# A fused decoder layer on one core: router work of the first token half two rounds earlier, last normalisations on ScalarE, router work of the second half one expert later

## The chip, the core and the metric

The kernel runs on one core of a Trainium2 chip. The time is the device time of one execution in microseconds (us). TensorE is called PE here, VectorE DVE, ScalarE ACT, GpSimd POOL and SyncE SP, as in the profile. Each engine runs its own list of instructions in order; they meet only at semaphores (a `then_inc` by one, a `wait_ge` by another).

## The reference, cut to what matters

```python
x = x + attn(layernorm(x))                       # local attention, blocks of 12 tokens
x = x + xattn(layernorm(x), ctx_1024)            # 16 heads, 512 context tokens, rope on the keys
x = x + ffn(layernorm(x))                        # the part that the change touches

def ffn(x, P_w, U1, U2, U3, W1, W2, b2):         # 1024 tokens of 128, 12 experts, top 3 of 12
    x_addr = x @ P_w.T                           # 64 wide
    dw1, dw2, dw3 = (route(x_addr @ U.T, 3) for U in (U1, U2, U3))   # softmax over the 3 largest
    h = sum(x @ W1[e].T * dw1[:, e:e+1] for e in range(12))          # 512 wide
    y = sum(gelu(h) @ W2[e].T * dw2[:, e:e+1] for e in range(12))
    return y + dw3 @ b2
```

The layer norms are over the last axis, without weights; the tokens are 4 batches of 256.

## The kernel before, in words

The 1024 tokens lie as 8 tiles of 128 in `x_sb`. After the local attention comes the cross attention: 4 batches times 16 heads, two heads at a time, so 32 **rounds** (`for r in range(NPAIR)`, one such loop on PE, ACT, DVE and POOL). A round r does, on PE and in this order: the scores of the next pair (L1075), a tile of values of a later group (`unit`, L901, up to round 27), in even rounds the queries of a later group (L1018 to L1020), the values weighed (L1092), the sum of weights (L1102), in some rounds (19, 21, 27, 29) a projection (L1111), a tile of keys (`unit`, L901, up to round 24) and the keys of pair r + 3 turned (L1004). ACT takes two exponentials (L749), copies the value tile (L670), the queries (L741) and the keys (L729). DVE divides the pair before (L1488, L1492), clips (L1481, two), and turns the key tile with rope (L1371, L1376). POOL sums the weights over key tiles (L519 two, L525 one) and adds the rope halves (L511).

Value tiles and key tiles, and the router, share one bank, 5, of the accumulator memory. So before its next use PE waits for the reader of the last: `rope_done` of DVE's L1376 after keys, `v_done` of ACT's L670 after values.

The last part is a mixture of experts on two halves of 512 tokens. The loop over n from 0 to 23 takes half 0 with its experts 0 to 11 and then half 1: `first_mixture(n)` (L1234 to L1236, 12 matmuls). Its input is made by DVE (`xeT`, L1520), ACT (`xeT_hi`, L763) and POOL (`xeT_lo`, L550, `token_rest`). Half 0 is ready for the final layer norm while the cross attention still runs, since its batches are done; half 1 is ready only after the projection of the last batch, which PE does behind `first_mixture(0)`.

Before a half can enter the mixture it goes through the **router**: statistics on DVE (`final_norm(half, 0)`, L1308, L1311), the reciprocal root on POOL (`rstd_of`, L468, L469), the normalisation (`final_norm(half, 1)`, L1314 on DVE), and stages `tokens` (4 transposes, L1154), `address` (L1158), `scores` (L1162, and on DVE the three largest), `chosen` and `softmax` (DVE), `turn` (4 transposes, L1167, then copies on ACT and DVE, and `gate_src`, which SP stores and spreads). A table `ROUTE` gives the half round of each stage for half 0, `ROUTE_2` the number n for half 1; an even entry 2r lies on PE ahead of the weighing of values of round r, an odd one at the end of the round. With the constants here `LAST_KEYS` is 24, so `ROUTE` runs from 49 (`weights`, the end of round 24) over 50, 52, 54, 56, 58 to 60 (round 30). `NORM_ROUND` is 23: statistics of half 0 in round 23, normalisation in round 24. On PE each stage in `ROUTE` first waits for `v_done` of the newest value tile; `weights` also waits for `rope_done` of all 32 key tiles:

```python
if i in ROUTE.values():
    pe.wait_ge(s["v_done"], min(i // 2 + V_LEAD, NG * KC - 1) + 1)
if i == ROUTE["weights"]:
    pe.wait_ge(s["rope_done"], NG * KC)
```

In half 1 POOL runs `token_rest(0)`, then `rstd_of`, then `token_rest(1)` and the rest, while DVE takes the statistics at n = 0 and normalises at n = 1.

Of the kernel before, what the change touches and what calls it, by code (L numbers as in the profile page):

```python
# [7 lines left out]
P = 128  # L8
# [15 lines left out]
def decoder_layer(nc, x, ctx_in, pos, a_wq, a_wk, a_wv, a_wpost, a_wrel, a_pds,  # L24
# [75 lines left out]
    with ExitStack() as ctx:  # L100
# [37 lines left out]
        def bank(i, parts=P):  # L138
# [10 lines left out]
        NSTAT = LN_F + NT  # L149
        stats = sb("stats", [P, NSTAT, 6])  # L150
# [121 lines left out]
            z_done fill_done top_done top3_done zr_done chosen_done zsh_done ez_done wsel_done zsum_done zrec_done  # L272
# [50 lines left out]
        def pv_bank(p):  # L323
# [5 lines left out]
        ROUTE = {"weights": 2 * LAST_KEYS + 1, "tokens": 2 * LAST_KEYS + 2, "address": 2 * LAST_KEYS + 4, "scores": 2 * LAST_KEYS + 6,  # L329
                 "chosen": 2 * LAST_KEYS + 8, "softmax": 2 * LAST_KEYS + 10, "turn": 2 * LAST_KEYS + 12}  # L330
        ROUTE_READ = {"weights": ("rt_done", 2), "tokens": ("fT_done", 1), "address": ("addr_done", 1), "scores": ("z_done", 1)}
        FILLED = 20
        NORM_ROUND = (B - 1) * PPB - 1

        ROUTE_2 = {"tokens": 3, "address": 4, "scores": 5, "chosen": 6, "softmax": 7, "turn": 8}

        HIDDEN = {NE: [(0, range(0, HC // 2))], NE + 1: [(0, range(HC // 2, HC))], 2 * NE - 1: [(1, range(HC))]}
        BIAS = {1: ("turn", 0), 2: ("product", 0), 9: ("turn", 1), 10: ("product", 1)}
# [117 lines left out]
        def _(pool):  # L456
# [102 lines left out]
            for r in range(NPAIR):  # L559
                for b, rounds in LATENT_ROUNDS.items():  # L560
                    for part in range(2):
                        if r == rounds[part]:
                            rstd_of(LN_1 + (2 * b + part) * TPB, TPB)
                if r + 1 < NPAIR:
                    weights_summed(2 * r + 2)
                    weights_summed(2 * r + 3)
                    halves_summed(r + 1)
                if r in ROUND_KEYS:
                    key_sum(r + K_LEAD)
                if r == NORM_ROUND:  # L570
                    rstd_of(LN_F, NT // 2)
                if r == FILLED:
                    pool.wait_ge(s["x1_done"], NT)
                    pool.memset(z[:, :, NE:NE + FILL], LOWEST).then_inc(s["fill_done"], 1)
                    pool.memset(top3[:, :, TOPK:8], LOWEST).then_inc(s["fill_done"], 1)
                    pool.memset(dw1T[:, :].bitcast(F32), 0.0).then_inc(s["fill_done"], 1)
                    pool.tensor_tensor(pick[:, :], ident[0:SPLIT, 0:NE], ident[0:SPLIT, REST:SPLIT], ALU.add).then_inc(s["pick_done"], 1)
                    pool.wait_ge(s["pick_done"], 1)
                    pool.tensor_copy(spread[:, :, :], pick[:, 0:GE, None].to_broadcast([SPLIT, GE, P])).then_inc(s["spread_done"], 1)

            token_rest(0)
            rstd_of(LN_F + NT // 2, NT // 2)
            for n in range(1, 2 * NE):
                token_rest(n)

        @block.scalar
        def _(act):
# [176 lines left out]

            def route(half, stage, at):
# [39 lines left out]
            for r in range(NPAIR):  # L805
# [24 lines left out]
            for n in range(2 * NE):  # L830
# [22 lines left out]
        def _(pe):  # L853
# [315 lines left out]

            def route_1(i):  # L1170
                if i in ROUTE.values():
                    pe.wait_ge(s["v_done"], min(i // 2 + V_LEAD, NG * KC - 1) + 1)
                if i == ROUTE["weights"]:
                    pe.wait_ge(s["rope_done"], NG * KC)
# [10 lines left out]
            for r in range(NPAIR):  # L1185
# [6 lines left out]
                if r in ROUND_VALUES:  # L1192
                    for stage, (read, count) in ROUTE_READ.items():
                        if ROUTE[stage] in (2 * r - 2, 2 * r - 1):
                            pe.wait_ge(s[read], count)
# [14 lines left out]
                if r in ROUND_KEYS:  # L1210
                    unit(ROUND_KEYS[r])
# [84 lines left out]
        def _(dve):  # L1296
# [225 lines left out]
            def final_norm(half, part):  # L1522
# [6 lines left out]
                else:  # L1529
                    dve.wait_ge(s["rstd_done"], 2 + B + 2 * B + half + 1)  # L1530
                    for i in range(4):
                        t = 4 * half + i
                        normalize(xn[:, t, :], x_sb[:, t, :], LN_F + t).then_inc(s["fn_done"], 1)
# [30 lines left out]
            def route_softmax(half):  # L1564
# [3 lines left out]
                dve.tensor_tensor(chosen[:, :, :], chosen[:, :, :], ez[:, :, :], ALU.mult).then_inc(s["wsel_done"], 1)  # L1568
                dve.wait_ge(s["wsel_done"], half + 1)
                dve.tensor_reduce(zsum[:, :], chosen[:, :, :], AX_X, ALU.add).then_inc(s["zsum_done"], 1)  # L1570
                dve.wait_ge(s["zsum_done"], half + 1)
                dve.reciprocal(zsum[:, :], zsum[:, :]).then_inc(s["zrec_done"], 1)
                dve.wait_ge(s["zrec_done"], half + 1)
# [26 lines left out]
            for r in range(NPAIR):  # L1600
                if r:
                    divide(r - 1)
                if r == NPAIR - 1:
# [20 lines left out]
                if r == NORM_ROUND:  # L1624
                    final_norm(0, 0)
                if r == NORM_ROUND + 1:
                    final_norm(0, 1)
                if r in ROUND_KEYS:
                    key_unit(ROUND_KEYS[r])
                route_1(2 * r + 1)  # L1630
# [3 lines left out]
            for n in range(2 * NE):  # L1634
# [4 lines left out]
                if n == 0:  # L1639
                    dve.wait_ge(s["tail_ps"], 1)  # L1640
                    for t in range(TPB):
                        tile = TPB * (B - 1) + t
                        dve.tensor_tensor(x_sb[:, tile, :], psum[:, 7, t * D:(t + 1) * D], x_sb[:, tile, :], ALU.add)\
                           .then_inc(s["x2_done"], 1)
                    final_norm(1, 0)
                if n == 1:
# [56 lines left out]
```

## Time and profile before

| | us |
|---|---|
| median of 3 runs (477.15 to 481.71) | 477.53 |
| the profiled execution | 475.94 |
| its span (first to last instruction) | 474.2 |
| PE busy in the span | 436.7 |
| DVE, POOL, ACT busy | 327.5, 244.6, 188.6 |

Everything that follows is read from the one profiled execution; positions are in us from the start of its span. PE is the engine on which nearly all of the chain that ended last lies (73% of it), so a row that shows PE idle shows time that the kernel loses, and a row of another engine matters if PE waits for it. A row of the timeline gives start, duration, engine, line, operation, what it writes and reads, and in square brackets how long the engine was idle just before and who ended that. The granted clock (PEclk) is 1.00 at the upper of its two levels, 2.4 GHz, and 0.50 at the lower, 1.2 GHz; a stretch in between held both.

### The profile page before, as it was taken

The page shows a single profiled execution, that of the slowest core. Times are in us where ns is not written, and L with a number is a line of the kernel's source. Part 1 is how long each engine was busy: PE and PEld are TensorE (multiplying, and loading weights), DVE is VectorE, ACT ScalarE, POOL GpSimd, SP SyncE. Part 2 cuts the span into 40 slices and gives each one's busy share as a digit, 9 for nine tenths or more (in the row PEclk, how much of TensorE's full clock was granted, in tenths as well). Part 3 has the DMA queues.
Part 4 walks back from the last instruction along what each step waited for, and adds up shares of the span by engine and source line. Part 5 has one row for each costly group of instructions (what it writes and reads, how often), then busy time and mean ns, then how long its engine had stood idle before and what let it go on. Part 6 is the DMA issues. An engine that isn't in the chain of part 4 may idle for free.

```text
span 474.2 us, 8559 instructions
## 1 busy us (share of the span) xinstructions
PE 436.7 (92%) x3264; PEld 321.7 (68%) x3264; DVE 327.5 (69%) x688; ACT 188.6 (40%) x296; POOL 244.6 (52%) x217
## 2 busy tenths in 40 slices
PE   3975899999999999989997989879999999999996
PEld 2653676766666766657765667558767788888885
DVE  8767578979998577896878579945553642465444
ACT  7648055546445454453443524314345432300000
POOL 5774138996898768877877544633332342000000
PEclk9999999999999999999998999998999999999999
DMA  6764321000000000000000000231425220000000
GB/s 167 183 143 70 60 85 45 0 1 1 0 1 2 1 1 1 0 1 2 1 1 2 1 0 1 80 123 45 134 82 187 103 98 0 3 11 7 11 6 11
DMA packets 32809, 19.83 MB, mean 42 GB/s; under 512 B 16437, under 2 KB 29674, under 8 KB 32770
## 3 DMA queue, kind: packets, MB, share of 16 engines
q1 hardware_dynamic: 32068, 19.02, 14.7%
q8 instruction: 26, 0.43, 0.4%
q10 hardware_dynamic: 702, 0.28, 0.2%
q14 instruction: 13, 0.11, 0.1%
HBM read 17.27 MB, written 2.02 MB: 41 GB/s over the span
## 4 chain that ended last, share of the span: by engine, by line
PE 73%; DVE 15%; ACT 6%; issue 4%; POOL 1%; DVEq 0%; ACTq 0%; POOLq 0%
PE psum L1092 10%; PE psum L1075 10%; PE psum L901 9%; PE psum L1271 5%; PE psum L1272 5%; PE psum L1270 5%; PE psum L1234 4%; PE psum L1236 4%; PE psum L1235 4%; PE psum L1111 3%; PE psum L1004 3%; PE psum L1102 2%; DVE rden L1488 2%; DVE kM L1383 2%; PE psum L1128 1%
## 5 line engine op out<-in xcount | busy, mean ns | idle before, releaser
L519 POOL TENSOR_TENSOR e_part<-e_sb 128x512 f32<-128x512 f32 x64 | 88.3, 1396 | 39.1 <-DVE e_sb L1481 39.1
L749 ACT ACTIVATE e_sb<-psum 128x1024 f32<-128x1024 f32 x64 | 62.4, 1023 | 22.2 <-PE psum L1075 22.2
L1075 PE MATMUL psum<-q_t,kT 64*128 64x256 f32 x512 | 65.6, 396 | 0.0
L1092 PE MATMUL psum<-e_sb,v_sb 128*64 128x256 f32 x512 | 62.9, 385 | 0.0
L1481 DVE TENSOR_SCALAR e_sb<-e_sb 128x1024 f32<-128x1024 f32 x64 | 56.1, 910 | 5.8 <-ACT e_sb L749 5.8
L1488 DVE RECIPROCAL rden<-psum 128x256 f32<-128x256 f32 x32 | 55.9, 1746 | 4.7 <-PE psum L1102 4.7
L1667 DVE SCALAR_TENSOR_TENSOR x_sb<-psum,dw,x_sb 128x128 f32<-128x128 f32 x96 | 33.7, 351 | 36.1 <-PE psum L1272 33.5
L550 POOL TENSOR_TENSOR xeT_lo<-xeT,xeT_hi 128x512 fp32r<-128x512 f32 x24 | 30.9, 1291 | 51.2 <-ACT xeT_hi L763 51.2
L1075 PEld LDWEIGHTS psum<-q_t,kT 64*128 64x128 f32 x512 | 48.1, 191 | 9.8 <-issue 5.4
L729 ACT ACTIVATE kT<-psum 128x512 f32<-128x512 f32 x32 | 19.2, 599 | 87.8 <-PE psum L1004 87.8
L511 POOL TENSOR_TENSOR k_rot<-rope_a,rope_b 128x512 f32<-128x512 f32 x32 | 42.3, 1322 | 16.8 <-DVE rope_b L1376 16.8
L1092 PEld LDWEIGHTS psum<-e_sb,v_sb 128*64 128x64 f32 x512 | 34.3, 136 | 21.4 <-issue 5.8
L1234 PE MATMUL psum<-xeT_hi,w1T_hi 128*128 128x512 f32 x96 | 40.3, 419 | 3.9 <-POOL xeT_lo L550 3.9
L525 POOL TENSOR_TENSOR e_part<-e_part 128x512 f32<-128x512 f32 x32 | 41.3, 1292 | 2.5
L1236 PE MATMUL psum<-xeT_hi,w1T_lo 128*128 128x512 f32 x96 | 38.4, 400 | 0.0
L1235 PE MATMUL psum<-xeT_lo,w1T_hi 128*128 128x512 f32 x96 | 38.1, 397 | 0.0
L1271 PE MATMUL psum<-w2T_lo,h_hi 128*128 128x512 f32 x96 | 38.0, 396 | 0.0
L763 ACT ACTIVATE xeT_hi<-xeT 128x512 fp32r<-128x512 f32 x24 | 15.1, 632 | 57.2 <-DVE xeT L1520 34.4
L1272 PE MATMUL psum<-w2T_hi,h_lo 128*128 128x512 f32 x96 | 37.8, 394 | 0.0
L1371 DVE TENSOR_TENSOR rope_a<-psum,cos_sb 128x512 f32<-128x512 f32 x32 | 22.0, 686 | 22.3 <-PE psum L901 21.9
L1270 PE MATMUL psum<-w2T_hi,h_hi 128*128 128x512 f32 x96 | 37.3, 389 | 0.0
L901 PE MATMUL psum<-wkv_hi,ctx_hi 128*128 128x512 f32 x64 | 31.5, 492 | 4.7 <-DVE rope_b L1376 4.7
(191 smaller groups left out, 778.0 us busy)
## 6 DMA issues: line engine op xcount, KB each, us to landing
w_raw<-in_L_ffn_W_dram SPq DMA_DIRECT2D x24, 256.0 KB, 2.7
gates<-gate_dram SPq DMA_DIRECT2D x6, 768.0 KB, 4.5
ctx_sb<-in_ctx_dram SPq DMA_DIRECT2D x4, 256.0 KB, 6.3
vbd<-v_dram SPq DMA_DIRECT2D x16, 52.6 KB
v_dram<-v_tok SPq DMA_DIRECT2D x4, 136.0 KB, 3.2
raw<-in_L_xattn_Wkv_dram SPq DMA_DIRECT2D x2, 256.0 KB, 5.6
k_rot<-in_L_xattn_Wkv_dram SPq DMA_DIRECT2D x2, 256.0 KB, 4.7
k_rot<-in_L_xattn_Wq_dram SPq DMA_DIRECT2D x2, 256.0 KB, 5.6
```

What stands on the lines that cost most here:

```text
L519: pool.tensor_tensor(e_part[:, p % 2, half, :, :], e_sb[:, i % ERING, :, 0, :], e_sb[:, i % ERING, :, 1, :], ALU.add)\
L749: act.activation(e_sb[:, i % ERING, :, :, :].rearrange("p a k t -> p (a k t)"), psum[:, a:a + 2, :].rearrange("p a b -> p (a b)"), ACT.Exp ...
L901: mm = pe.matmul(o, c, w_[:, wc:wc + GC], start=(part == 0), stop=(part == 2))
L1075: mm = pe.matmul(psum[:, 2 * (i % 2) + a, t * S:(t + 1) * S], kT[rows, p % 3, kt * P:(kt + 1) * P], q_t[rows, j % 2, p % 2, :], start=True ...
L1092: mm = pe.matmul(psum[DX * a:DX * a + DX, pv_bank(p), 0:S], v_sb[g % 2][:, kt, 2 * pp + a, :], e_sb[:, i % ERING, a, t, :], start=(kt == 0 ...
L1234: pe.matmul(bank(c), w1T_hi[:, e, c, :], hi, start=(e == 0), stop=False)
L1235: pe.matmul(bank(c), w1T_hi[:, e, c, :], lo, start=False, stop=False)
L1236: mm = pe.matmul(bank(c), w1T_lo[:, e, c, :], hi, start=False, stop=(e == NE - 1))
L1270: pe.matmul(o, hi, w_hi, start=(c == 0), stop=False)
L1271: pe.matmul(o, hi, w_lo, start=False, stop=False)
L1272: mm = pe.matmul(o, lo, w_hi, start=False, stop=(c == HC - 1))
L1488: dve.reciprocal(rden[:, p % 2, :], psum[:, pv_bank(p), S:2 * S]).then_inc(s["rden_done"], 1)
```

## The change

The diff, cut to its core (the rest renames three semaphores into one, adds the tile `nm` of 128 x 8 and moves a loop into a function):

```diff
-        ROUTE = {"weights": 2 * LAST_KEYS + 1, "tokens": 2 * LAST_KEYS + 2, "address": 2 * LAST_KEYS + 4, "scores": 2 * LAST_KEYS + 6,
-                 "chosen": 2 * LAST_KEYS + 8, "softmax": 2 * LAST_KEYS + 10, "turn": 2 * LAST_KEYS + 12}
+        NORM_ROUND = (B - 1) * PPB - 2
+        ROUTE = {"weights": 2 * NORM_ROUND, "tokens": 2 * NORM_ROUND + 2, "address": 2 * NORM_ROUND + 4, "scores": 2 * NORM_ROUND + 6,
+                 "chosen": 2 * NORM_ROUND + 8, "softmax": 2 * NORM_ROUND + 10, "turn": 2 * NORM_ROUND + 12}
-        NORM_ROUND = (B - 1) * PPB - 1
-        ROUTE_2 = {"tokens": 3, "address": 4, "scores": 5, "chosen": 6, "softmax": 7, "turn": 8}
+        ROUTE_2 = {"tokens": 4, "address": 5, "scores": 6, "chosen": 7, "softmax": 8, "turn": 9}
-        BIAS = {1: ("turn", 0), 2: ("product", 0), 9: ("turn", 1), 10: ("product", 1)}
+        BIAS = {1: ("turn", 0), 2: ("product", 0), 10: ("turn", 1), 11: ("product", 1)}
...
+                if r == NORM_ROUND:
+                    rstd_of(LN_F, NT // 2)
                 if r in ROUND_KEYS:
                     key_sum(r + K_LEAD)
-                if r == NORM_ROUND:
-                    rstd_of(LN_F, NT // 2)
...
-            token_rest(0)
-            rstd_of(LN_F + NT // 2, NT // 2)
-            for n in range(1, 2 * NE):
+            for n in range(2 * NE):
                 token_rest(n)
+                if n == 2:
+                    rstd_of(LN_F + NT // 2, NT // 2)
...
+            def final_normalize(half):
+
+                act.wait_ge(s["nm_done"], half + 1)
+                for t in range(4 * half, 4 * half + 4):
+                    act.activation(xn[:, t, :], x_sb[:, t, :], ACT.Identity, scale=rstd[:, LN_F + t:LN_F + t + 1], bias=nm[:, t:t + 1])\
+                       .then_inc(s["fn_done"], 1)
...
                 route_1(2 * r + 1)
+                if r == NORM_ROUND:
+                    final_normalize(0)
...
+                if n == 3:
+                    final_normalize(1)
...
                 if i == ROUTE["weights"]:
-                    pe.wait_ge(s["rope_done"], NG * KC)
...
                 if r in ROUND_KEYS:
+                    route_read(2 * r)
                     unit(ROUND_KEYS[r])
...
-                    for i in range(4):
-                        t = 4 * half + i
-                        normalize(xn[:, t, :], x_sb[:, t, :], LN_F + t).then_inc(s["fn_done"], 1)
+                    at = slice(4 * half, 4 * half + 4)
+                    st = slice(LN_F + 4 * half, LN_F + 4 * half + 4)
+                    dve.scalar_tensor_tensor(nm[:, at], mv[:, st, 0], -1.0, rstd[:, st], ALU.mult, ALU.mult).then_inc(s["nm_done"], 1)
...
                 if r:
                     divide(r - 1)
+                if r == NORM_ROUND:
+                    final_norm(0, 0)
...
-                if r == NORM_ROUND:
-                    final_norm(0, 0)
-                if r == NORM_ROUND + 1:
-                    final_norm(0, 1)
                 if r in ROUND_KEYS:
                     key_unit(ROUND_KEYS[r])
+                if r == NORM_ROUND:
+                    final_norm(0, 1)
...
+                if n == 1:
                     final_norm(1, 0)
-                if n == 1:
+                if n == 3:
                     final_norm(1, 1)
```

`NORM_ROUND` is now 22, and `ROUTE` runs over 44, 46, 48, 50, 52, 54 and 56: `weights` in round 22, `tokens` in 23, `address` in 24, `scores` in 25, `chosen` in 26, `softmax` in 27, `turn` in 28. The normalisation (x - m) * rstd becomes x * rstd + nm with nm = -m * rstd; DVE makes the four columns of `nm` in one small instruction, and ACT normalises the four tiles. `route_read` is the old wait ahead of a tile that overwrites a router result, now also ahead of key tiles.

The order of ACT's instructions in rounds 22 and 23, before (e_sb are the exponentials, v_sb a value tile, q_t the queries, kT turned keys; round 23 begins with the second row of e_sb):

```order
L749 ACTIVATE e_sb<-psum 128x1024 [waits part_done,pv_ps,score_ps] x2
L670 ACTIVATE v_sb<-psum 128x512 [waits pv_ps,unit_ps]
L741 ACTIVATE q_t<-psum 128x512 [waits score_ps,misc_ps]
L729 ACTIVATE kT<-psum 128x512 [waits score_ps,misc_ps]
L749 ACTIVATE e_sb<-psum 128x1024 [waits part_done,pv_ps,score_ps] x2
L670 ACTIVATE v_sb<-psum 128x512 [waits pv_ps,unit_ps]
L729 ACTIVATE kT<-psum 128x512 [waits score_ps,misc_ps]
```

And of the change, the same two rounds on ACT:

```order
L750 ACTIVATE e_sb<-psum 128x1024 [waits part_done,pv_ps,score_ps] x2
L671 ACTIVATE v_sb<-psum 128x512 [waits pv_ps,unit_ps]
L742 ACTIVATE q_t<-psum 128x512 [waits score_ps,misc_ps]
L807 ACTIVATE pwT<-psum 128x64 [waits rt_ps]
L808 ACTIVATE uT<-psum 64x36
L730 ACTIVATE kT<-psum 128x512 [waits score_ps,misc_ps]
L770 ACTIVATE xn<-x_sb,nm,rstd 128x128 [waits nm_done]
L770 ACTIVATE xn<-x_sb,nm,rstd 128x128 x3
L750 ACTIVATE e_sb<-psum 128x1024 [waits part_done,pv_ps,score_ps] x2
L671 ACTIVATE v_sb<-psum 128x512 [waits pv_ps,unit_ps]
L776 ACTIVATE xnT<-psum 128x512 [waits fT_ps]
```

The normalisation now stands on ACT ahead of the exponentials and the value copy of round 23.

DVE's instructions of round 22 in the change, from the division to the next division (`nm` is the new small one):

```order
L1504 RECIPROCAL rden<-psum 128x256 [waits ox_done,den_ps]
L1508 TENSOR_TENSOR o_t<-psum,rden 128x256 [waits rden_done]
L1324 BN_STATS stats<-x_sb 128x6 [waits misc_read]
L1324 BN_STATS stats<-x_sb 128x6 x3
L1327 BN_AGGR mv<-stats 128x2 [waits stats_done]
L1327 BN_AGGR mv<-stats 128x2 x3
L1497 TENSOR_SCALAR e_sb<-e_sb 128x1024 [waits exp_done] x2
L1387 TENSOR_TENSOR rope_a<-psum,cos_sb 128x512 [waits k_rot_done,unit_ps]
L1392 TENSOR_TENSOR rope_b<-psum,sin_sb 128x8x32 x2
L1549 SCALAR_TENSOR_TENSOR nm<-mv,rstd 128x4 [waits rstd_done]
L1504 RECIPROCAL rden<-psum 128x256 [waits ox_done,den_ps]
```

Before, the statistics stood in round 23 behind the two clips (e_sb), and nothing of the router stood in round 22.

POOL at the start of the mixture, before (from the first `token_rest`):

```order
L550 TENSOR_TENSOR xeT_lo<-xeT,xeT_hi 128x512 [waits pv_ps,xeT_hi_done]
L468 TENSOR_SCALAR veps<-mv 128x4 [waits mv_done]
L469 TENSOR_TENSOR rstd<-veps,neghalf 128x4 [waits chain_pool]
L550 TENSOR_TENSOR xeT_lo<-xeT,xeT_hi 128x512 [waits xeT_hi_done] x2
L550 TENSOR_TENSOR xeT_lo<-xeT,xeT_hi 128x512 [waits h_ps,xeT_hi_done] x21
```

And of the change:

```order
L551 TENSOR_TENSOR xeT_lo<-xeT,xeT_hi 128x512 [waits pv_ps,xeT_hi_done]
L551 TENSOR_TENSOR xeT_lo<-xeT,xeT_hi 128x512 [waits xeT_hi_done] x2
L469 TENSOR_SCALAR veps<-mv 128x4 [waits mv_done]
L470 TENSOR_TENSOR rstd<-veps,neghalf 128x4 [waits chain_pool]
L551 TENSOR_TENSOR xeT_lo<-xeT,xeT_hi 128x512 [waits h_ps,xeT_hi_done] x21
```

The reciprocal root of half 1 moved behind two more `token_rest`.

## Rows read from the trace of the kernel before

**Rows 1.** The page: busy time and share of the span by engine.

```profile
PE 436.7 (92%) x3264; PEld 321.7 (68%) x3264; DVE 327.5 (69%) x688; ACT 188.6 (40%) x296; POOL 244.6 (52%) x217
```

**Rows 2.** Windows: stretch, length, busy PE, PEld, DVE, ACT, POOL; PEclk, DMA, GB/s.

```profile
226.00:254.00 28.00, 28.00 (x208) 19.82 (x208) 22.68 (x39) 13.32 (x18) 22.89 (x23) 1.00 0.01 2
254.00:261.00 7.00, 4.07 (x23) 3.48 (x23) 5.97 (x8) 1.60 (x4) 3.47 (x3) 0.76 0.00 0
...
318.00:323.00 5.00, 4.35 (x12) 3.45 (x13) 3.19 (x6) 1.58 (x3) 3.11 (x3) 0.66 0.01 2
```

**Rows 3.** Timeline of PE, rounds 23 to 25: start, duration, what [idle before].

```profile
241.36 2.00 PE L1075 MATMUL psum<-q_t,kT 64*128 64x256 f32 x16
...
244.18 1.95 PE L1092 MATMUL psum<-e_sb,v_sb 128*64 128x256 f32 x16
...
257.99 0.34 PE L1177 MATMUL psum<-ident,pw_sb 64*128 64x64 f32 x1 [2.93 <-issue]
...
258.19 3.37 PE L1075 MATMUL psum<-q_t,kT 64*128 64x256 f32 x15
...
263.18 0.66 PE L1154 MATMUL psum<-ident,xn 128*128 128x128 f32 x4 [0.73 <-ACT v_sb L670]
```

**Rows 4.** Timeline of DVE, rounds 22 to 24.

```profile
237.27 1.28 DVE L1481 TENSOR_SCALAR e_sb<-e_sb 128x1024 f32<-128x1024 f32 x2
...
241.64 0.75 DVE L1376 TENSOR_TENSOR rope_b<-psum,sin_sb 128x256 f32<-128x256 f32 x2
...
245.63 0.86 DVE L1308 BATCH_NORM_STATS2 stats<-x_sb 128x6 f32<-128x128 f32 x4
246.53 0.38 DVE L1311 BATCH_NORM_AGGREGATE mv<-stats 128x2 f32<-128x6 f32 x4
...
252.49 4.13 DVE L1314 TENSOR_SCALAR xn<-x_sb,mv,rstd 128x128 f32<-128x128 f32 x4 [0.33 <-POOL rstd L469]
...
257.14 0.74 DVE L1376 TENSOR_TENSOR rope_b<-psum,sin_sb 128x256 f32<-128x256 f32 x2
```

**Rows 5.** Timeline of POOL, rounds 22 to 24.

```profile
238.03 2.88 POOL L519 TENSOR_TENSOR e_part<-e_sb 128x512 f32<-128x512 f32 x2 [1.45 <-DVE e_sb L1481]
240.99 1.27 POOL L525 TENSOR_TENSOR e_part<-e_part 128x512 f32<-128x512 f32 x1
...
250.64 0.24 POOL L468 TENSOR_SCALAR veps<-mv 128x4 f32<-128x4 f32 x1
250.96 1.49 POOL L469 TENSOR_TENSOR rstd<-veps,neghalf 128x4 f32<-128x4 f32 x1
```

**Rows 6.** Timeline of ACT, round 23.

```profile
242.54 1.94 ACT L749 ACTIVATE e_sb<-psum 128x1024 f32<-128x1024 f32 x2 [0.47 <-PE psum L1075]
244.37 0.60 ACT L670 ACTIVATE v_sb<-psum 128x512 f32<-128x512 f32 x1
```

**Rows 7.** Groups of ACT by form: shape, count, busy us, mean ns, idle before.

```profile
L652 ACT ACTIVATE ctx_f<-psum,affine 128x512 f32<-128x512 f32 x4 | 3.1, 782 | 0.2 <-PE psum L879 0.2
...
L713 ACT ACTIVATE lat_f<-psum,affine 128x256 f32<-128x256 f32 x4 | 2.3, 567 | 6.7 <-PE psum L991 6.7
```

**Rows 8.** Timeline of PE, from round 27 to the third expert.

```profile
277.74 1.08 PE L1162 MATMUL psum<-uT,addrT 64*128 64x36 f32 x8 [0.77 <-ACT v_sb L670]
...
302.75 0.46 PE L1144 MATMUL psum<-dw1T,spread 44*128 44x512 f32 x1 [1.23 <-ACT gate_src L783]
...
314.66 0.60 PE L1247 MATMUL psum<-ident,dw 128*12 128x128 f32 x4
318.65 0.50 PE L1234 MATMUL psum<-xeT_hi,w1T_hi 128*128 128x512 f32 x1 [3.39 <-POOL xeT_lo L550]
...
324.70 0.50 PE L1234 MATMUL psum<-xeT_hi,w1T_hi 128*128 128x512 f32 x1
```

**Rows 9.** Timeline of POOL at the second expert.

```profile
316.32 1.04 POOL L469 TENSOR_TENSOR rstd<-veps,neghalf 128x4 f32<-128x4 f32 x1
317.33 2.50 POOL L550 TENSOR_TENSOR xeT_lo<-xeT,xeT_hi 128x512 fp32r<-128x512 f32 x2
```

More of the change, by code:

```diff
@@ L149, in decoder_layer @@
         NSTAT = LN_F + NT
+        nm = sb("nm", [P, NT])
         stats = sb("stats", [P, NSTAT, 6])
@@ L271, in decoder_layer @@
             ld_pw ld_u ld_b2 wt_ps wt_hi_done wt_lo_done rt_ps rt_done fn_done fT_ps fT_done addr_ps addr_done z_ps
-            z_done fill_done top_done top3_done zr_done chosen_done zsh_done ez_done wsel_done zsum_done zrec_done
+            z_done fill_done top_done top3_done zr_done chosen_done zsh_done ez_done wsum_done nm_done
             dw_done pick_done spread_done gate_src_done gate_stored ld_gate0 ld_gate1 dw1_ps dw1_hi_done dw1_lo_done dw3_ps dw3_done spread_ps xe_done
@@ L1168, in route, with route_read @@
                     mm.then_inc(s["dw1_ps"], 1)
+            def route_read(i):
+                for stage, (read, count) in ROUTE_READ.items():
+                    if ROUTE[stage] == i:
+                        pe.wait_ge(s[read], count)
             def route_1(i):
@@ L1192, in _ @@
                 if r in ROUND_VALUES:
-                    for stage, (read, count) in ROUTE_READ.items():
-                        if ROUTE[stage] in (2 * r - 2, 2 * r - 1):
-                            pe.wait_ge(s[read], count)
+                    route_read(2 * r - 2)
                     unit(ROUND_VALUES[r])
@@ L1567, in route_softmax @@
                 dve.wait_ge(s["ez_done"], half + 1)
[L1568 to L1573, printed above, removed]
+                dve.tensor_tensor(chosen[:, :, :], chosen[:, :, :], ez[:, :, :], ALU.mult).then_inc(s["wsum_done"], 1)
+                dve.wait_ge(s["wsum_done"], 3 * half + 1)
+                dve.tensor_reduce(zsum[:, :], chosen[:, :, :], AX_X, ALU.add).then_inc(s["wsum_done"], 1)
+                dve.wait_ge(s["wsum_done"], 3 * half + 2)
+                dve.reciprocal(zsum[:, :], zsum[:, :]).then_inc(s["wsum_done"], 1)
+                dve.wait_ge(s["wsum_done"], 3 * half + 3)
                 dve.tensor_tensor(dw[:, half, :, :, :].rearrange("p i r e -> p (i r) e"), chosen[:, :, :],
```

## The prediction

> **What bounds the kernel now.** I read the page first: PE is busy for 436.7 of 474.2 us [rows 1], so the question is only where PE idles or runs slowly, and what the change does there. The windows come next. From 226 to 254 (rounds 21 to 24) PE is busy for all 28.00 us at granted clock 1.00, while POOL has 22.89, DVE 22.68 and ACT 13.32; from 254 to 261 it has only 4.07 of 7.00 at 0.76, and from 318 to 323 the clock is 0.66 [rows 2]. Only the timeline tells why.
>
> First hole: PE idles 2.93 us ahead of the `weights` transposes at the end of round 24 [rows 3]. The row says "issue", but DVE tells the cause: the four normalisations take 4.13 us, the rope of the last key tile stands behind them and ends at 257.88 (257.14 + 0.74) [rows 4], and PE waits for `rope_done`. The next scores take 3.37 us for 15 where 16 took 2.00 [rows 3]: the clock fell behind the hole, and that costs another 1.4.
>
> Second hole: PE idles 3.39 us ahead of the second expert [rows 8]. POOL makes rstd of half 1 (316.32, 1.04 us) ahead of `xeT_lo` of that expert [rows 9], and rstd had to wait for the last batch. Again the clock falls: 5 us at 0.66 lack 1.7 us of full speed [rows 2].
>
> Smaller ones: 0.73 and 0.77 us in rounds 25 and 27, where a router stage in an odd round waits for ACT's value copy [rows 3, 8], and 1.23 for `gate_src` [rows 8]. The even round in between shows no such wait, because the queries fill PE meanwhile.
>
> **The change, part by part.** The sum is made on the profiled execution, 475.94 us; the median 477.53 lies 1.6 above it, and I carry this difference over.
>
> *Taken away in rounds 24 to 31.* The wait for `rope_done` (2.93), its slow clock (1.4), the wait in round 25 (0.73; what takes its place is counted below), and the 1.23 for `gate_src`, since `turn` now lies two rounds ahead of its user. Together 6.3 us.
>
> *Round 22.* The transposes of `weights` are only moved (about 0.3 us of PE work either way). Their wait for the value copy falls into an even round, behind the queries: I take 0.1, between 0 and the 0.73 of an odd round.
>
> *Round 23, the term that decides.* `tokens` now waits in round 23 for the value copy of that round. On ACT this copy stands behind two exponentials, and these behind `final_normalize(0)`, which waits for `nm`, `rstd` and the statistics. I follow the chain in the old timeline:
> - The statistics, 1.28 us (245.63 to 246.91) [rows 4], now stand ahead of the clips of round 22. These begin at 237.27 + 1.28 = 238.55.
> - POOL begins its sums 0.76 behind the first clip and ends the third 4.23 later (238.03 to 242.26) [rows 5]: 239.31 to 243.54.
> - rstd takes 1.81 from the start of veps to its end (250.64 to 252.45) beside the clips [rows 5], 1.36 with the 1.04 of an undisturbed one [rows 9]: 244.9 to 245.35. DVE has done its rope by 242.39 (241.64 + 0.75) [rows 4] and waits there, so I lean to the lower. The little `nm` and two semaphores: 0.25 (an estimate; it is smaller than any DVE row shown).
> - ACT, four tiles. The nearest rows have scale and bias from memory too: 0.782 for 512 elements and 0.567 for 256, so 0.46 for 128 [rows 7]. Two neighbours overlap by 0.11 (the copy starts at 244.37, the exponentials end at 244.48) [rows 6]: 4 x 0.46 - 0.33 = 1.5. ACT is free at 246.65 to 247.1.
> - Exponentials of round 23 and value copy: 1.83 + 0.60 [rows 6]. The copy is done at 249.1 to 249.5.
>
> PE gets there at 244.18 [rows 3] plus the 0.3 and 0.1 of round 22: 244.6. It waits 4.5 to 4.9 us; I take 4.7. What queues behind PE is everything, for the weighing of values stands behind `tokens`. ACT would have been done at 244.97 without the normalisation. After two holes of 2.93 and 3.39 the clock was down; after this one I expect the same and add 1.4, the smaller of 1.4 and 1.7.
>
> By the section "What's actually happening" of the page "TensorE: Matmul & The Clock Gate" in the Trainium skill, the clock is at half rate by default and only activity lifts it. This speaks against the change, which puts the longest idle stretch into rounds without any. The trace agrees with both drops [rows 2], and without this fall the sum would be 1.4 lower.
>
> *Round 24 to 28.* `address` moves from one even round into another, `scores` from odd to odd (0.77 stays). `chosen` lies in an even round; `softmax` does nothing on PE but still waits for `v_done` in round 27, an odd one: 0.75 new. DVE has lost 4.13 us of normalisation and both statistics and maxima lie in rounds as long as before, so I cost them at nothing: PE's own round covers them, and DVE's 22.68 busy of 28 [rows 2] leave a fifth of each round free; if this cover is gone, each us that DVE is late costs one.
>
> Rounds 22 to 31 together: 0.1 + 4.7 + 1.4 + 0.75 - 6.3 = **+0.65**.
>
> *Start of the mixture.* `token_rest(1)` and `(2)` no longer stand behind rstd, so the second expert starts when PE is there, at 315.26 (314.66 + 0.60) [rows 8]: -3.39, and -1.7 for the clock. What is late next? DVE now takes the statistics at n = 1, behind the work of the fourth expert, and POOL runs rstd ahead of `token_rest(3)`. Statistics would be ready at about 318.5 (an estimate: what DVE and ACT do for an expert, some 2.6 us behind 314.6, then 1.28), rstd 1.36 later, `xeT_lo` 1.25 after that [rows 9]: 321.1. PE needs it after two experts. From the second to the third it took 324.70 - 318.65 = 6.05, less 1.7 for the clock 4.35 [rows 8], and the next is shorter by the bias product, some 3.3: 322.9. It is 1.8 us early. The four normalisations on ACT at n = 3 end close to where PE wants to turn the tokens at n = 4; I put 0.2 there. Everything of half 1 behind it moves with its consumers by one expert: nothing. Together **-4.9**.
>
> **Sum.** +0.65 - 4.9 = -4.25: 471.7 for an execution like the profiled one, and 477.53 - 4.25 = **473.3 us** for the median.
>
> A rule touches the 4.7. rstd took 1.49 us beside clips and 1.04 with DVE idle [rows 5, 9]. The page "SBUF — State Buffer" of the Trainium skill, section "Who interferes with whom", has DVE and GpSimd share a port pair that one of them holds for its whole instruction, the other blocked. By that rule the short 1.04 would hold in round 22, where DVE stands still, and the sum would be 0.2 lower; by the midpoint of the two rows it is as above. The two rows agree with the rule, but cannot say that a port did it.
>
> **The rivals.**
> *A, the forecast (0.57):* a hole in round 23 of 4 to 5.5 us with its slow clock, the hole at the second expert gone. 475.94 - 4.25; its own range for the median is 471.8 to 475.2.
> *B, round 23 costs little (0.20):* the chain through POOL is shorter, since POOL has 1.45 us idle ahead of its sums [rows 5], or the clock holds. If the hole is under about 2.5 us, so that only 2.5 remain of 6.1, the gain is 4.25 + 3.6 = 7.9: 469.7. If the clock alone holds, 471.9. Against it: the 1.45 are ahead of the clips, which slip themselves.
> *C, the hole at the experts comes back two later (0.12):* rstd ahead of `token_rest(3)`, if the statistics are ready more than 1.8 us later than I reckon. A wait as long as the old (3.39) with its 1.7 gives back 5.1: +0.85, a median of **478.4**, slower than before. The margin of 1.8 speaks against it, and a tight ring of buffers that chains DVE, ACT and POOL speaks for it.
> *D, round 23 costs more (0.11):* the lag on DVE and POOL is carried on and PE waits again in rounds 24 and 25, or the slow clock lasts through two rounds (another 1.5 to 3): 475 to 476.3.
> That the change does not do what it says is left out: the order of ACT and POOL in the change shows the moves.
>
> **How the numbers follow.** The range takes A, most of B and of D, and leaves out C and the deep end of B: 470.3 to 476.6. A measurement of this kernel can tell about 1%, 4.8 us, from no change. Faster by more needs a gain over 4.8: all but a little of B (0.18) and the upper part of A, where the hole is near 4 us (0.17), so 0.35. Slower by over 1% would need C and D together: 0.03. The rest is 0.62.
>
> **What would show it.** Right: in round 23 a PE row of 4 transposes of `xn` with about 4.7 us idle before it, ended by ACT's value copy, and scores or weighing behind it at half clock; four ACT rows of 128x128 at about 0.46 us; no wait ahead of the `pw_sb` transposes; the second expert's first matmul directly behind the `dw` transposes; 0.75 idle in round 27. Wrong: that wait under 3 us (B); idle PE ahead of the fourth expert's first matmul, ended by `xeT_lo` (C); waits for DVE or POOL in rounds 24 to 26 (D).

## The result, and the profile of the changed kernel

| | before | changed |
|---|---|---|
| median, us (20 runs each) | 476.99 | 475.02 |
| lowest to highest, us | 474.4 to 481.71 | 472.83 to 477.88 |
| the profiled execution, us | 475.94 | 472.83 |
| its span, us | 474.2 | 471.1 |

The ratio is 0.9949, with a 95% interval of 0.9926 to 0.9972: the changed kernel is faster by 0.5%, 2.0 us by the medians. (All ratios in this document leave out executions more than 1.5% above the fastest of their kernel.) The forecast was 473.3 us within 470.3 to 476.6, a gain of 4.25 us. The profiled execution of the changed kernel is the fastest of its twenty, so the 3.1 us between the two profiles flatter the change. The page and four windows of the changed kernel (columns as in [rows 2]: PE, PEld, DVE, ACT, POOL busy, granted clock, DMA share, GB/s):

```profile
PE 436.0 (93%) x3264; PEld 320.0 (68%) x3264; DVE 323.7 (69%) x682; ACT 191.9 (41%) x304; POOL 245.5 (52%) x217
```

```profile
226.00:254.00 28.00, 22.51 (x159) 15.44 (x155) 18.56 (x30) 11.70 (x20) 18.92 (x20) 0.88 0.00 1
254.00:261.00 7.00, 6.94 (x48) 4.98 (x48) 4.64 (x7) 4.23 (x6) 2.99 (x3) 1.00 0.02 4
250.00:255.00 5.00, 5.00 (x28) 2.93 (x27) 0.86 (x1) 0.60 (x1) 2.84 (x3) 0.70 0.00 0
318.00:323.00 5.00, 5.00 (x28) 4.03 (x28) 3.78 (x16) 1.51 (x3) 2.99 (x4) 1.00 0.25 73
```

Against [rows 2], the picture has turned round. The 28 us that PE had filled at full clock now lack 5.5 us of PE, at 0.88; the hole behind 254 and the slow stretch at 318 are gone. PE's timeline of the changed kernel, all of its waits from round 22 to the fifth expert but one of 0.48 us that stood there before:

```profile
249.69 1.12 PE L1166 MATMUL psum<-ident,xn 128*128 128x128 f32 x4 [5.43 <-ACT v_sb L671]
250.73 3.04 PE L1104 MATMUL psum<-e_sb,v_sb 128*64 128x256 f32 x16
...
267.29 1.08 PE L1174 MATMUL psum<-uT,addrT 64*128 64x36 f32 x8 [0.77 <-ACT v_sb L671]
...
281.43 1.95 PE L1104 MATMUL psum<-e_sb,v_sb 128*64 128x256 f32 x16 [0.77 <-ACT v_sb L671]
...
306.84 0.65 PE L1114 MATMUL psum<-e_part,ones 128*64 128x256 f32 x4 [0.42 <-POOL e_part L526]
...
309.04 0.50 PE L1250 MATMUL psum<-xeT_hi,w1T_hi 128*128 128x512 f32 x1 [0.30 <-POOL xeT_lo L551]
...
316.23 0.60 PE L1263 MATMUL psum<-ident,dw 128*12 128x128 f32 x4
316.58 0.47 PE L1250 MATMUL psum<-xeT_hi,w1T_hi 128*128 128x512 f32 x1
```

One hole of 5.43 us ahead of the tokens' transposes in round 23, weighing behind it at 3.04 us where [rows 3] had 1.95 to 2.00 for as many matmuls, and a second expert that starts without a wait (3.39 in [rows 8]).

To compare kernels I cut each profile at two points that all of them have: the first score matmul of round 22 and the first `w1T_hi` matmul of the first expert. That leaves out the start of the program, where executions of one kernel differ by more than the edits do.

| kernel | round 22 starts | round 22 to first expert | first expert to end |
|---|---|---|---|
| before | 234.20 | 73.29 | 166.71 |
| changed | 233.83 | 75.21 | 162.06 |

The difference is -0.37 ahead of round 22, +1.92 in the rounds and -4.65 in the mixture; the forecast had 0, +0.65 and -4.9. A second profile of the changed kernel gave 75.35 and 161.95, so the last two stretches repeat within 0.15 us.

### The profile page after: what moved, and what is told of

The parts are those of the page before. It is cut to its first block, busy times and chain, and to the rows that moved or that the text cites. A ratio compares the mean times of both kernels' runs of the same rounds, so it can differ in the third digit from the quotient of the medians.

```text
span 471.1 us, 8560 instructions
## 1 busy us (share of the span) xinstructions
PE 436.0 (93%) x3264; PEld 320.0 (68%) x3264; DVE 323.7 (69%) x682; ACT 191.9 (41%) x304; POOL 245.5 (52%) x217
## 4 chain that ended last, share of the span: by engine, by line
PE 71%; DVE 15%; ACT 8%; issue 4%; POOL 2%; DVEq 0%; ACTq 0%; POOLq 0%
PE psum L1104 11%; PE psum L1087 9%; PE psum L913 8%; PE psum L1287 5%; PE psum L1288 5%; PE psum L1286 5%; PE psum L1250 3%; PE psum L1123 3%; PE psum L1252 3%; PE psum L1251 3%; PE psum L1114 3%; PE psum L1016 3%; ACT e_sb L750 2%; DVE kM L1399 2%; DVE rden L1504 1%
## 5 line engine op out<-in xcount | busy, mean ns | idle before, releaser
L1104 PE MATMUL psum<-e_sb,v_sb 128*64 128x256 f32 x512 | 64.0, 390 | 0.8 <-ACT v_sb L671 0.8
L1087 PE MATMUL psum<-q_t,kT 64*128 64x256 f32 x512 | 64.2, 389 | 0.0
L1087 PEld LDWEIGHTS psum<-q_t,kT 64*128 64x128 f32 x512 | 46.8, 186 | 9.9 <-issue 5.6
```

The costliest lines, as they stand in the source:

```text
L1087: mm = pe.matmul(psum[:, 2 * (i % 2) + a, t * S:(t + 1) * S], kT[rows, p % 3, kt * P:(kt + 1) * P], q_t[rows, j % 2, p % 2, :], start=True ...
L1104: mm = pe.matmul(psum[DX * a:DX * a + DX, pv_bank(p), 0:S], v_sb[g % 2][:, kt, 2 * pp + a, :], e_sb[:, i % ERING, a, t, :], start=(kt == 0 ...
```

## Experiments

Each kernel here was timed in 5 to 12 executions and profiled in one; a ratio stands against the kernel before on the same chip. The stretches at the end of this section are cut as above.

**One part of the change alone.** One kernel has the first half's share of the change without the second's, another has it the other way round. The core of the first one's edit against the changed kernel, and of the second one's:

```diff
-        ROUTE_2 = {"tokens": 4, "address": 5, "scores": 6, "chosen": 7, "softmax": 8, "turn": 9}
+        ROUTE_2 = {"tokens": 3, "address": 4, "scores": 5, "chosen": 6, "softmax": 7, "turn": 8}
-                if n == 2:
+                if n == 0:
                     rstd_of(LN_F + NT // 2, NT // 2)
```

```diff
-        ROUTE = {"weights": 2 * NORM_ROUND, "tokens": 2 * NORM_ROUND + 2, "address": 2 * NORM_ROUND + 4, "scores": 2 * NORM_ROUND + 6,
+        ROUTE = {"weights": 2 * LAST_KEYS + 1, "tokens": 2 * LAST_KEYS + 2, "address": 2 * LAST_KEYS + 4, "scores": 2 * LAST_KEYS + 6,
...
-        NORM_ROUND = (B - 1) * PPB - 2
+        NORM_ROUND = (B - 1) * PPB - 1
```

> The first half's router in rounds 22 to 28 with its normalisation on ScalarE, the second half as before. Theory (the two parts add up, and the first one costs): a hole of 5.4 us on TensorE ahead of the token transposes of round 23, the first expert 1.9 us later than before counted from round 22 on, and the hole of 3.4 us at the second expert as before: 1.5 to 2.0 us slower than before. Rival (the first part pays, the second one is what disappoints): faster than before by 1 us or more.

> The kernel before with only the second half's part of the change (reciprocal root behind two more xeT_lo, statistics at n = 1, normalisation on ScalarE at n = 3, router stages one expert later). Theory: the hole of 2.9 us in round 24 stays, the one of 3.4 us at the second expert is gone with its slow clock: 4.5 to 5 us faster than before, faster than the whole change by 1.5 to 2.5. Rival (the parts need each other, the gain is the shorter way of the first half): within 2 us of before.

Measured: the first half's share alone 480.81 us, ratio 1.0061 (1.0027 to 1.0094); the second half's alone 473.05 us, 0.9917 (0.9883 to 0.9951). By its ratio the first is 2.9 us slower (1.3 to 4.5), more than the 1.5 to 2.0 expected but with them inside the interval; the second is faster as expected. By stretches the first costs 75.15 - 73.29 = +1.86 and leaves the mixture at 166.77; the second leaves the rounds at 73.43 and takes the mixture to 161.96. The holes stay with their parts. PE's timeline of the first-half kernel, then of the second-half one:

```profile
252.23 1.11 PE L1164 MATMUL psum<-ident,xn 128*128 128x128 f32 x4 [5.42 <-ACT v_sb L671]
253.27 3.01 PE L1102 MATMUL psum<-e_sb,v_sb 128*64 128x256 f32 x16
...
322.70 0.50 PE L1248 MATMUL psum<-xeT_hi,w1T_hi 128*128 128x512 f32 x1 [3.40 <-POOL xeT_lo L551]
```

```profile
259.51 0.34 PE L1187 MATMUL psum<-ident,pw_sb 64*128 64x64 f32 x1 [2.93 <-issue]
...
259.72 3.50 PE L1085 MATMUL psum<-q_t,kT 64*128 64x256 f32 x15
```

So the change is two changes that don't meet. One gains 4.7 us, the other gives 1.9 back.

**The rope sum held back.** In the changed kernel DVE's `nm`, 4 numbers a partition, takes 1.22 us, and POOL's rope sum began 0.06 us before it. Here POOL waits for `nm`:

```diff
                     rstd_of(LN_F, NT // 2)
+                    pool.wait_ge(s["nm_done"], 1)
```

> The change, with one more wait: in round 22 GpSimd waits for nm before its next rope sum. Theory (VectorE's nm, two inputs from SBUF, took 1.22 us because GpSimd's rope sum had begun 0.06 us earlier): nm falls to about 0.2 us, ScalarE begins the four normalisations 1.0 us earlier, the hole in round 23 goes from 5.4 to 4.4 us, and the time falls by about 1.0 us against the change. Rival (nm is slow by itself, for its strided operand): nm stays at 1.2 us, GpSimd only waits longer, and the time is that of the change or up to 0.5 us more.

The timeline of the changed kernel, DVE and then POOL:

```profile
244.43 1.22 DVE L1549 SCALAR_TENSOR_TENSOR nm<-mv,rstd 128x4 f32<-128x4 f32 x1 [2.03 <-POOL rstd L470]
```

```profile
243.35 1.04 POOL L470 TENSOR_TENSOR rstd<-veps,neghalf 128x4 f32<-128x4 f32 x1
244.37 1.26 POOL L512 TENSOR_TENSOR k_rot<-rope_a,rope_b 128x512 f32<-128x512 f32 x1
```

And of this one, DVE, POOL and PE:

```profile
249.27 0.16 DVE L1550 SCALAR_TENSOR_TENSOR nm<-mv,rstd 128x4 f32<-128x4 f32 x1 [2.04 <-POOL rstd L470]
```

```profile
249.51 1.26 POOL L512 TENSOR_TENSOR k_rot<-rope_a,rope_b 128x512 f32<-128x512 f32 x1 [0.28 <-DVE nm L1550]
```

```profile
253.47 1.11 PE L1167 MATMUL psum<-ident,xn 128*128 128x128 f32 x4 [4.37 <-ACT v_sb L672]
254.51 3.68 PE L1105 MATMUL psum<-e_sb,v_sb 128*64 128x256 f32 x16
```

`nm` falls from 1.22 to 0.16 us and the hole from 5.43 to 4.37, by the same 1.06. This shows that the POOL instruction held `nm`. The time does not follow, against what was expected: 474.89 us, ratio 0.9946 (0.9919 to 0.9973), against 475.02, and the rounds take 75.44. In the profiled execution the clock took it back. Windows of this kernel:

```profile
253.50:256.00 2.50, 2.50 (x12) 1.60 (x14) 1.15 (x1) 0.60 (x1) 1.86 (x2) 0.50 0.00 0
256.00:258.00 2.00, 2.00 (x14) 1.05 (x12) 0.00 (x0) 0.00 (x0) 1.26 (x1) 0.50 0.00 0
258.00:260.00 2.00, 2.00 (x9) 1.05 (x6) 0.00 (x0) 0.00 (x0) 0.00 (x0) 0.61 0.00 0
260.00:262.00 2.00, 2.00 (x19) 1.67 (x19) 1.77 (x4) 0.86 (x2) 0.34 (x1) 1.00 0.00 0
```

PE works here for 6.5 us at 0.50 to 0.61 (2.50, 2.00 and 2.00 us) and lacks 1.25 + 1.0 + 0.78 = 3.0 us of full clock; the changed kernel lacks 5 x 0.30 = 1.5 behind its longer hole (250 to 255 at 0.70). That is one execution of each, and this one, of 477.82 us, is the slowest of its kernel; the medians, equal within 0.13 us, fit it but don't prove it for the others.

**Another engine, another order.** In the next three the `tokens` step stays in round 23. First, DVE makes the first half's normalisations, in round 22 where `nm` was; ACT keeps the second half's:

```diff
+                    if half == 0:
+                        for t in range(4):
+                            normalize(xn[:, t, :], x_sb[:, t, :], LN_F + t).then_inc(s["fn_done"], 1)
+                        return
```

> The change, with the four normalisations of the first half back on VectorE (at the place of nm in round 22), those of the second half on ScalarE. Theory (ScalarE is the wrong engine here, since its exponentials and value copy of round 23 queue behind the normalisations): ScalarE copies the value at 245.0 as before, TensorE waits in round 23 only for VectorE, which is held by GpSimd's rope sum for 1.3 us and then needs 1.1: done near 246.9, a hole of 2.7 us instead of 5.4, faster than the change by 2.5 to 4 us. Rival (the hole is set by the statistics and GpSimd, whatever engine normalises): a hole of 4.5 us or more, within 1 us of the change.

Then ACT keeps them, behind the exponentials and the value copy of round 23 and not ahead of them; the last one has POOL's wait for `nm` as well:

```diff
                     value_unit(ROUND_VALUES[r])
+                if r == NORM_ROUND + 1:
+                    final_normalize(0)
...
-                if r == NORM_ROUND:
-                    final_normalize(0)
```

> The change, with ScalarE's four normalisations moved from the end of round 22 behind the value copy of round 23. Theory: the exponentials and the value copy run as before (copy done at 245.0), the normalisations then from 245.7 (nm is still held) to 247.3, and TensorE's hole in round 23 is 3.1 us instead of 5.4: about 2.3 us faster than the change, the slow clock behind the hole as before (1.4 us). Rival (a hole of 3 us is short enough for the clock to hold in this place): 3.7 us faster than the change and a granted clock of 1.00 behind it.

> The same, and GpSimd waits for nm before its rope sum in round 22. Theory: normalisations from 245.1 (the value copy ends then) to 246.7, a hole of about 2.3 us, 0.7 us less than without the wait; if the clock falls behind this one too, 3 us faster than the change, if it holds, 4.5. Rival (nm is slow by itself): as without the wait.

| kernel | median us | ratio | hole |
|---|---|---|---|
| on DVE | 470.55 | 0.9834 (0.9789 to 0.988) | 1.60 |
| ACT, value copy first | 472.62 | 0.9886 (0.9838 to 0.9933) | 2.07 |
| the same, POOL waits | 470.58 | 0.9844 (0.9786 to 0.9902) | 1.24 |

PE's timeline and a window of the kernel on DVE:

```profile
246.97 1.00 PE L1164 MATMUL psum<-ident,xn 128*128 128x128 f32 x4 [1.60 <-DVE xn L1328]
247.90 3.28 PE L1102 MATMUL psum<-e_sb,v_sb 128*64 128x256 f32 x16
```

```profile
248.00:251.00 3.00, 3.00 (x18) 1.72 (x20) 2.88 (x4) 0.60 (x1) 0.61 (x1) 0.56 0.00 0
```

The same two views of the last one, value copy first and POOL waiting:

```profile
246.64 1.38 PE L1167 MATMUL psum<-ident,xn 128*128 128x128 f32 x4 [1.24 <-ACT xn L771]
247.94 2.99 PE L1105 MATMUL psum<-e_sb,v_sb 128*64 128x256 f32 x16
```

```profile
248.00:251.00 3.00, 3.00 (x19) 1.81 (x20) 1.06 (x2) 0.60 (x1) 2.46 (x2) 0.62 0.00 0
```

The long hole was thus the queue on ACT: four normalisations ahead of two exponentials and the copy that PE waits for. With another order on the same engine 3.4 us of it go. All three holes came about 1.1 us shorter than expected, in part since PE starts on the first tile; that part of the wait moved in between the four transposes, which take 1.00, 1.54 and 1.38 us (in the order of the table) where four take 0.66 without a wait. Yet the clock still falls behind these short holes, to 0.56 and 0.62. Over 4 us (248 to 252, 251 to 255 and 248 to 252) it is 0.57, 0.57 and 0.59, so 1.6 to 1.7 us of full clock are lacking. The intervals of the ratios of these three overlap, so the times do not rank them.

**The chain one round earlier.** This kernel takes the statistics in round 21, `rstd` ahead of POOL's sums in round 22, `nm` behind the clips, and the normalisations on ACT ahead of the key copy and so of the exponentials:

```diff
-                if r == NORM_ROUND:
-                    final_norm(0, 0)
...
+                if r == NORM_ROUND - 1:
+                    final_norm(0, 0)
```

> The change, with the chain of the first half begun earlier: statistics in round 21 behind the last projection, reciprocal root first on GpSimd in round 22, nm behind the clips, ScalarE's four normalisations in round 22 ahead of the keys. Theory (the hole of 5.4 us in round 23 is only the length of this chain ahead of ScalarE's exponentials): the hole shrinks to the 0.75 us of any odd round, no slow clock behind it, and the time falls by 5 to 6 us against the change, about 8 us against before. Rival (VectorE and GpSimd are too full in rounds 21 and 22): the hole goes, but waits of 1 to 3 us for the rope or the sums appear in rounds 21 to 23, and less than 4 us are gained against the change.

469.21 us, ratio 0.9832 (0.9804 to 0.986), rounds 68.99. PE's timeline of it and a window:

```profile
248.78 0.66 PE L1166 MATMUL psum<-ident,xn 128*128 128x128 f32 x4 [0.76 <-ACT v_sb L671]
249.36 1.95 PE L1104 MATMUL psum<-e_sb,v_sb 128*64 128x256 f32 x16
```

```profile
247.00:252.00 5.00, 4.24 (x30) 2.55 (x29) 2.43 (x4) 2.32 (x4) 3.66 (x4) 1.00 0.00 0
```

The hole is down to the 0.76 of any odd round, and no clock is lost: 75.21 - 68.99 = 6.2 us, of which 4.67 are hole and the rest is the clock's 1.5. The 0.76 of round 23 is PE's wait for the value copy, as in rounds 25 and 27. Without the wait for the value copy at `chosen` and `softmax`, which do nothing on PE, on top of it:

```diff
-                if i in ROUTE.values():
+                if i in [ROUTE[k] for k in ("weights", "tokens", "address", "scores", "turn")]:
                     pe.wait_ge(s["v_done"], min(i // 2 + V_LEAD, NG * KC - 1) + 1)
```

> The kernel with the early chain of the first half, and without the wait of TensorE for the value copy in the stages chosen and softmax, which have no instruction on TensorE. Theory: the 0.77 us idle in round 27 goes, and its followers come earlier by as much: 0.6 to 0.8 us faster than the early kernel. Rival (that wait is covered by another, for the clips or the sums of weights): no change, the idle time moves to the next wait of round 27.

467.96 us, ratio 0.9791 (0.9739 to 0.9842), rounds 68.03: the 0.77 of round 27 is gone. The stretch is 0.96 shorter, and the other 0.2 was not taken apart; the two ratios overlap, so only the traces tell the two kernels apart. Its median is the lowest of all kernels here.

**The hole of before, by one swap.** The prediction read the 2.93 us ahead of `weights` as DVE's queue: rope behind normalisations. The second-half kernel still has this hole, and one swap in it tests the reading:

```diff
-                if r == NORM_ROUND + 1:
-                    final_norm(0, 1)
                 if r in ROUND_KEYS:
                     key_unit(ROUND_KEYS[r])
+                if r == NORM_ROUND + 1:
+                    final_norm(0, 1)
```

> As half2_only (the second half's steps moved and on ScalarE, the first half's left where they were before), with one more edit: in round 24 VectorE's half of the key rope of that round goes ahead of the first half's normalisation, which had held it for 4.13 us. Reading of the hole before the change: the four matmuls of round 24 waited for that normalisation only because the key rope stood behind it in VectorE's queue. If so, the 2.93 us hole shrinks to at most 1.5 us, TensorE's clock keeps its full step, and the time falls by 2.93 - 1.1 and some 1.6 us of slow clock, to 468 to 470.5 against half2_only's 473.05. The other reading: the hole is the normalisation's own length and is only put off to the scores or the transposes of the first routing step: then a hole of 2 to 3 us stands a little later and the time stays at 472 to 474.

469.25 us, ratio 0.9803 (0.9763 to 0.9844), rounds 70.01 for 73.43. Its timeline of DVE and of PE, and windows:

```profile
254.84 0.74 DVE L1386 TENSOR_TENSOR rope_b<-psum,sin_sb 128x256 f32<-128x256 f32 x2
255.50 2.21 DVE L1324 TENSOR_SCALAR xn<-x_sb,mv,rstd 128x128 f32<-128x128 f32 x4
```

```profile
255.69 0.24 PE L1187 MATMUL psum<-ident,pw_sb 64*128 64x64 f32 x1 [1.05 <-issue]
```

```profile
254.00:255.70 1.70, 0.65 (x6) 0.40 (x4) 1.47 (x4) 0.60 (x1) 1.62 (x2) 1.00 0.00 0
255.70:258.00 2.30, 2.30 (x19) 1.97 (x20) 2.30 (x5) 1.31 (x4) 1.41 (x2) 1.00 0.00 0
```

`rope_b` ends at 255.58 and PE goes on at 255.69, with the normalisations only begun: PE had waited for the rope, not for them. The hole shrinks by 1.88 and the clock stays at 1.00, which is the other 1.5 of 73.43 - 70.01 = 3.42. By the medians this kernel, which has the second half's share as well, is 8.8 us under the kernel before on that chip (478.05), where the whole change is 3.0 under it.

**The changed kernel once more,** beside this one on the same chip:

> The changed kernel itself once more, so that it stands beside half2_keyfirst and the kernel before on one chip. If the parts add up as they did, it stays at 0.993 to 0.997 of the kernel before. If the gain is only a matter of which executions a set happens to hold, its interval takes in 1.

475.08 us, ratio 0.9937 (0.9908 to 0.9967), as expected. One of its twelve executions took 1072.4 us at a granted clock of 1.00; no trace of it was kept, and why is open. Its profile has the hole at 5.42, `nm` at 1.22, rounds 75.35 and mixture 161.95.

| kernel | round 22 starts | round 22 to first expert | first expert to end |
|---|---|---|---|
| first half's share alone | 236.38 | 75.15 | 166.77 |
| second half's alone | 235.71 | 73.43 | 161.96 |
| the same, rope ahead of normalisations | 233.76 | 70.01 | 161.93 |
| rope sum held back | 238.68 | 75.44 | 161.98 |
| value copy first | 238.47 | 72.33 | 162.00 |
| the same, POOL waits | 234.98 | 71.78 | 161.94 |
| on DVE | 234.94 | 71.85 | 161.91 |
| chain one round earlier | 237.57 | 68.99 | 161.94 |
| the same, one wait less | 236.89 | 68.03 | 161.98 |

## Why the forecast came out, and where its steps did not

**Mixture: right.** -4.65 for -4.9, and [rows 8] and [rows 9] were the right place to read it. The second expert follows its `dw` transposes at once. The rest is what was priced as the next late thing, rival C. The timeline of the changed kernel, POOL and then PE:

```profile
319.93 0.58 POOL L469 TENSOR_SCALAR veps<-mv 128x4 f32<-128x4 f32 x1 [6.31 <-DVE mv L1327]
320.59 1.04 POOL L470 TENSOR_TENSOR rstd<-veps,neghalf 128x4 f32<-128x4 f32 x1
321.60 2.54 POOL L551 TENSOR_TENSOR xeT_lo<-xeT,xeT_hi 128x512 fp32r<-128x512 f32 x2
```

```profile
324.26 0.48 PE L1250 MATMUL psum<-xeT_hi,w1T_hi 128*128 128x512 f32 x1
...
327.56 1.26 PE L1166 MATMUL psum<-ident,xn 128*128 128x128 f32 x4
```

The first of the two `xeT_lo` ends at 321.60 + 1.27 = 322.9, and PE takes it at 324.26: a margin of 1.4 where 1.8 was forecast. No wait, so C did not happen, in any of the kernels with this part. The tokens' transposes of the second half cost more than forecast. They take 1.26 us, and the next expert begins 1.04 us after their start, where it was 0.60 and 0.36 before: 0.7 more for a forecast of 0.2, since they follow ACT tile by tile. Of these 0.5 the rest of the mixture gives back half, which was not taken apart, and 0.25 is missing.

**Rounds: the places right, two sizes too small.** Forecast +0.65, measured +1.92.
- *Taken away:* all of it. `weights` waits for nothing in round 22, so its 0.1 was 0; `gate_src` no longer shows; 0.77 stays in round 25 and one of 0.77 is new in round 27 (forecast 0.75).
- *The hole:* 5.43 for 4.7. Step by step, in the changed kernel's own positions, which lie 0.37 earlier at round 22. Clips begin at 238.09 (forecast 238.55 - 0.37 = 238.18); POOL's sums end at 243.07 (243.17); rstd ends at 244.39 (244.5 to 245.0); PE stops at 249.69 - 5.43 = 244.26 (244.23). All lie within 0.15 us of the forecast or of its near end: rstd took 1.04 us, the shorter of the two rows that the forecast lay between. Then the estimate that had no row: from rstd's end to ACT's first normalisation 1.29 us pass, not 0.25. ACT's rows of the changed kernel:

```profile
245.68 1.66 ACT L770 ACTIVATE xn<-x_sb,nm,rstd 128x128 f32<-128x128 f32 x4 [3.61 <-DVE nm L1549]
247.24 1.91 ACT L750 ACTIVATE e_sb<-psum 128x1024 f32<-128x1024 f32 x2
249.05 0.58 ACT L671 ACTIVATE v_sb<-psum 128x512 f32<-128x512 f32 x1
```

The four tiles take 1.66 (forecast 1.5), exponentials and copy end 2.4 later, as reckoned. ACT's start comes 1.04 late by this term and 0.36 early against the middle of the range for rstd's end, which is the 0.73 within 0.05. So the failed term is "The little `nm` and two semaphores: 0.25": +1.04. It was sized by how little it computes, while the next instruction on POOL, the rope sum, starts at the same moment as `nm`. The prediction had even named the rule that covers it, and used it on rstd alone. That page, "SBUF — State Buffer" of the Trainium skill, section "Who interferes with whom", says that a DVE instruction with two SBUF inputs contends with a GpSimd instruction that reads SBUF; `nm` reads `mv` and `rstd`, and 1.22 against 0.16 us agree.
- *The clock:* 1.5 from 250 to 255 for a forecast of 1.4.
- *Not forecast:* 0.42 at the end of the attention (306.84, for `e_part`). Nothing stood there before; POOL's sums are on the path now that `gate_src` no longer holds PE. That takes back a third of the 1.23.

The terms: +0.73 hole, +0.1 clock, +0.42 at the end, -0.1 for `weights`, make 1.15 of the 1.27 missing. One more term was not forecast and goes the other way: PE's wait for `xeT_lo` ahead of the first expert, 0.56 before (at 307.49) and 0.30 now (at 309.04), takes 0.26 off. So some 0.4 of the rounds stays unexplained.

**The rivals.** B (a short hole, or the clock holds) was no case of this kernel, but its price was wrong as well: it let the slow clock go together with the hole. Holes of 1.24 to 2.07 us still cost it. D priced POOL and DVE waits in rounds 24 to 26: there are none. The longer slow clock that D named happened only in the kernel with the rope sum held back.

**The range and the median.** For an execution like the profiled one the forecast was 471.7, and 472.83 came: 1.27 + 0.25 from the terms, less the 0.37 ahead of round 22. For the median it was 473.3, and 475.02 came: 0.6 more is the 1.6 that I carried over from profile to median, which is 2.2 for the changed kernel. That is inside A's own range (471.8 to 475.2), at its upper end.

The number came out better than the sum did. The gain was forecast at 4.25 us and measured at 2.0 by the medians, 2.7 by the two stretches (+1.92 - 4.65) and 3.1 by the profiles. The range of 6.3 us was wider than the gain, and it started from a median of 477.53 over 3 executions, where 20 gave 476.99; from that one the forecast would be 472.7, which is 2.3 us short. The two places, their waits and what ended them were foreseen; that the time fell inside the range is in part luck.

**What stays open.** Why the clock falls behind one short hole and not behind another is open. It kept 1.00 behind holes of 0.76 and 1.05 us, and in the kernel before behind the 1.23 of [rows 8]; it fell behind 1.24 with 0.7 more between the transposes (1.38 for 0.66). The kernel before, where PE waits for `gate_src` until 302.75:

```profile
300.00:307.00 7.00, 5.70 (x41) 2.91 (x37) 6.60 (x9) 1.70 (x3) 4.98 (x4) 1.00 0.29 81
```

So the length of the hole alone does not tell the two apart. Why the shorter hole of 4.37 was followed by twice the loss of the 5.43 one was not settled either; where each hole fell in time differs between all of these kernels.

## To carry to other kernels

Read a hole as a queue: behind the two long holes of the rounds PE waited not for the normalisations but for the short work queued behind them (rope on DVE, value copy on ACT), and one swap of two calls was worth 3.4 us where the whole change was worth 2.7 by the same stretches. Time a change's parts apart: here -4.7 and +1.9 were added into a gain that hardly measures. And size a small instruction on a critical chain by what the neighbour engine starts in the same moment, not by its elements.

## What the runs showed of the hardware

- A `scalar_tensor_tensor` of 128x4 takes 0.16 us on DVE alone and 1.22 or 1.23 beside a POOL `tensor_tensor` of 1.26 us that began just before it. The same four normalisations on DVE (128x128) took 1.11 us in the second half of the kernel before, while POOL was idle (322.40 to 324.61):

```profile
322.16 1.11 DVE L1314 TENSOR_SCALAR xn<-x_sb,mv,rstd 128x128 f32<-128x128 f32 x4
```

  They took 2.05 in round 22 of the kernel on DVE, beside one POOL instruction of 1.26 us; 2.21 in the kernel with the rope first, beside two; and 4.13 in [rows 4], where POOL's sums ran beside them for 3.8 us. So most of the 4.13 that held the rope of before looks like waiting for POOL and not work. No run tests that.
- A hole of 1.24 to 1.6 us, with short gaps behind it, was followed by 3 us at a granted clock of 0.56 to 0.62; holes of 0.76, 1.05 and 1.23 were followed by 1.00. The loss of full clock behind a hole did not grow with the hole (1.7 us behind 1.24, 3.0 behind 4.37, 1.5 behind 5.43).
- Executions of one kernel differ with the mean granted clock, by 1.1% in the changed kernel and 1.5% in the one before: the changed kernel took 472.8 to 473.7 us at 0.986 and above, and 477.0 to 477.9 at 0.975 and below. In the profiles the difference lies in the first 80 us: 0.96 there and round 22 at 233.83 in the changed kernel, 0.85 and 238.68 in the one with the rope sum held back. The two profiles of the changed kernel agree within 0.14 us in each of the two stretches used here. So a comparison of two single executions here is worth little under 5 us, and the stretch between two common points is worth more.
